# One accumulator instead of two for the sums of the first edge layer

## The reference, cut to what matters

```python
h = (layernorm(x) @ W.T).reshape(N, 8, 32)
alpha = leaky_relu(einsum(h[src], a_src) + einsum(h[dst], a_dst))          # one per edge and head
exp_a = exp(alpha - segment_max(alpha, dst)[dst])
seg_sum = segment_sum(exp_a, dst)
agg = segment_sum(h[src] * (exp_a / max(seg_sum[dst], 1e-10)), dst)
x = x + agg.reshape(N, 256) + bias
x = x + ffn(layernorm(x)); ...
```

## Time and profile before

| what | value |
|---|---|
| median of 3 runs | 1845.91 us (1844.1 to 1847.94) |
| profiled execution, its own time | 1847.34 us |
| its span in the profile | 1845.6 us |
| busy in the span: PE, DVE, ACT, POOL | 1307.0, 1403.1, 935.2, 1085.2 us |
| first edge layer (63 to 640 us): PE, DVE, ACT, POOL busy | 337.0, 477.7, 300.8, 424.1 us |
| Vector's adds in it (L936) | 416 |
| Vector's busy time of 640 to 680 us, the first mixing | 33.5 us |

### The profile page before, as it was taken

The page is one execution under the profiler, slowest core; times in us unless marked ns, Lnnn a source line. Parts: engine busy times, 40 slices in busy tenths (PEclk is TensorE's granted clock), DMA queues, the critical chain, the costliest instruction groups (busy, mean ns, idle before and its releaser), DMA issues. The chain is left out here.

```text
span 1845.6 us, 29221 instructions
## 1 busy us (share of the span) xinstructions
PE 1307.0 (71%) x7043; PEld 921.3 (50%) x7043; DVE 1403.1 (76%) x3587; ACT 935.2 (51%) x3225; POOL 1085.2 (59%) x1146
## 2 busy tenths in 40 slices
PE   6346656665566468999795787877787878867086
PEld 5234434443344366777453455555555555456075
DVE  6558888888889962544867899999999999675444
ACT  3345555545545352332351476777777777346043
POOL 3677777777777200000416777777777777474556
PEclk9668777777777758999997799999999999876588
DMA  5566666667666209200247888888888888436392
GB/s 151 157 186 209 206 215 204 206 208 208 214 205 198 85 1 321 81 1 1 91 171 254 261 262 259 250 267 264 273 263 271 253 270 255 136 114 154 142 333 65
DMA packets 168854, 353.60 MB, mean 192 GB/s; under 512 B 27831, under 2 KB 64776, under 8 KB 168564
## 3 DMA queue, kind: packets, MB, share of 16 engines
q0 software_dynamic: 58192, 175.85, 31.4%
q1 hardware_dynamic: 106501, 172.46, 28.7%
q10 hardware_dynamic: 4000, 3.41, 0.6%
HBM read 268.43 MB, written 87.33 MB: 193 GB/s over the span
## 5 line engine op out<-in xcount | busy, mean ns | idle before, releaser
L827 POOL DMA_INDIRECT e_rows<-h_rows,src_col x416 | 414.8, 997 | 136.8 <-issue 123.4
L1345 POOL DMA_INDIRECT e_rows<-kv_rows,src_col x320 | 307.0, 959 | 101.2 <-issue 67.3
L1104 PE MATMUL e_sum<-e_rows,e_of_dst 128*128 128x264 f32 x832 | 294.5, 497 | 85.6 <-DVE e_rows L926 78.3
L1564 ACT ACTIVATE e_rows<-e_rows 128x64 f32<-128x64 f32 x1152 | 281.4, 336 | 0.3
L1627 PE MATMUL e_query<-q,e_to_dst 128*128 x1248 | 203.6, 295 | 75.1 <-DVE e_rows L1398 56.9
L1104 PEld LDWEIGHTS e_sum<-e_rows,e_of_dst 128*128 128x128 f32 x832 | 177.7, 240 | 126.1 <-DVE e_rows L926 82.2
L1667 PE MATMUL e_sum<-e_rows,e_of_dst 128*128 128x260 f32 x640 | 187.4, 416 | 1.3 <-POOL e_rows L1274 0.7
L1627 PEld LDWEIGHTS e_query<-q,e_to_dst 128*128 128x128 bf16 x1248 | 120.2, 100 | 131.4 <-issue 92.0
L1029 ACT ACTIVATE e_rows<-e_rows 128x32 f32<-128x32 f32 x832 | 181.0, 305 | 0.1
L1486 DVE TENSOR_TENSOR acc<-acc,e_sum 128x260 f32 x346 | 145.5, 420 | 42.1 <-DVE acc L1486 19.4
L1345 POOL DMA_INDIRECT x<-kv_rows,src_col x96 | 91.7, 955 | 73.4 <-POOLq L2149 39.8
(11 more groups left out here) (429 smaller groups left out, 2728.5 us busy)
## 6 DMA issues: line engine op xcount, KB each, us to landing
step_of<-e_of_dst SPq DMA_DIRECT2D x104, 256.0 KB, 2.2
e_of_dst<-step_of SPq DMA_DIRECT2D x104, 256.0 KB
sorted_rows<-zeros SPq DMA_DIRECT2D x1, 14560.0 KB
comb<-sorted_rows SPq DMA_DIRECT2D x56, 260.0 KB
e_rel<-step_rel SPq DMA_DIRECT2D x26, 512.0 KB, 4.3
step_to<-e_to_dst SPq DMA_DIRECT2D x26, 512.0 KB, 5.7
e_to_dst<-step_to SPq DMA_DIRECT2D x52, 256.0 KB
e_rows<-h_rows,src_col POOLq DMA_INDIRECT x416, 3.3
```

Source lines behind the costliest of these rows:

```text
L827: pool.indirect_dma_start(out=g[t // BATCH % R][:, t % BATCH, :], out_offset=None, in_=k.h_rows[:, :], in_offset=bass.IndirectOffsetOnAxis ...
L1104: pe.matmul(psm[t % NB], of_dst[q][:, s % GROUP, :], g[m % R][:, s, :], start=True, stop=True).then_inc(summed, 1)
L1345: pool.indirect_dma_start(out=rows_at(t, 1)[:, 0, :], out_offset=None, in_=k.kv_rows[:, :], in_offset=bass.IndirectOffsetOnAxis(ap=k.src_c ...
L1564: ins = act.activation(x, x, ACT.Copy, scale=row[:, plo + h:plo + h + 1])
```

## The change

`acc0_odd` goes away. `edges_first` gets a list of one accumulator, so it clears and rescales one, all steps are added to it, and `len(accs)` in the wait of `add` is 1: add t waits until add t-1 has ended, where it waited for add t-2. In `mix_first` the two additions per round go away, and the bound reads the sums in the accumulator directly.

```diff
-                c.inc(v.tensor_tensor(inv[b][:, :, :], k.acc0[:, at, D:R0], k.acc0_odd[:, at, D:R0], ALU.add))
-                summed = c.count
-                c.inc(v.tensor_tensor(vals, vals, k.acc0_odd[:, at, 0:D], ALU.add))
-                v.wait_ge(k.dve_steps, summed)
-                c.inc(v.tensor_scalar(inv[b][:, :, :], inv[b][:, :, :], 1e-10, None, ALU.max))
+                c.inc(v.tensor_scalar(inv[b][:, :, :], k.acc0[:, at, D:R0], 1e-10, None, ALU.max))
...
             k.acc0 = sb(stage, "acc0", [P, WIN, R0])
-            k.acc0_odd = sb(stage, "acc0_odd", [P, WIN, R0])
             with ExitStack() as inner:
-                edges_first(nc, k, a, inner, [k.acc0, k.acc0_odd])
+                edges_first(nc, k, a, inner, [k.acc0])
```

## The result

| | before | after |
|---|---|---|
| median, 6 runs each | 1844.7 us | 1854.84 us |
| span of the profiled execution | 1845.6 us | 1854.3 us |
| score row of batch 2 | 128.31 | 129.69 |
| score row of batch 24 | 585.34 | 596.21 |
| first mixing starts | 636.74 | 651.31 |

The kernel is slower: ratio 1.0057, 95% interval 1.0039 to 1.0075, 10.1 us by the medians. It was forecast slower, by 4.5 us to 1850.4. The time lies in the range of 1846 to 1857, in its upper part, and above the 1848.7 to 1853.5 that the prediction called its forecast. In the profiled executions the edge stage ends 14.6 us later and the mixing gives 2.7 back. Of the 11.9 us then open the profiled span keeps 8.7: the stages behind, which the change does not touch, took 3.2 us less in this execution.

The account below looks back on a forecast made before the run. The gathers were taken to set the steady pace, Vector having some air and bounding the end. Edge stage +7.1 us less 2.6 in the mixing gave +4.5 on 1845.9: 1850.4 us, forecast 1848.7 to 1853.5, range 1846 to 1857.

Parts of the forecast that it names:

- steady part: First edge layer, batches 2 to 24: Vector's 456.2 us nearly tie with the gathers' 457.0, so nearly nothing is paid.
- the 2.45 us behind batch 22: After the last full gather wait, two laps without air put batch 24's score row at 587.8 instead of 585.34.
- The new wait: Neighbouring adds into the one accumulator start 0.63 us apart instead of 0.34, costing 0.29 us per direct neighbour.
- rival C: The added waits cost nothing, as the skill says; laps of 18.3 us stay behind the gathers; 1841.5 us; chance 0.08.
- One lap: A Vector lap gains 2.14 us from add waits and loses 0.42 of rescale: 1.72 longer, 20.42 us.
- rival A: Vector becomes the bound outright as idle time before the rescale grows; 1862.6 us, 1854.9 with half; chance 0.15.
- B: Rival: the gathers go on hiding all and only the tail counts; 1847.5 to 1848.7 us; chance 0.20.
- the chance of "slower": Chance 0.53 of measurably slower: two thirds of the forecast's range, lying above the 3.7 us resolution, with rival A.
- The tail: Last laps of the edge stage, where nothing hides Vector: with the 2.45 us before it, the stage ends 7.1 us later.
- the lock (2.8): Tail comparison beside GpSimd's multiplications: an exclusive port lock blocks the loser, so its end moves by 2.8 us.
- the share (3.4): Alternative for the same comparison: Vector and GpSimd share the time, and it ends 0.6 us later, 3.4.
- The mixing: First mixing: five merging additions vanish, two of them on the path, saving 2.6 us (bounds 1.5 to 3.0).

Follow-up runs that it names:

- e1: Kernel before (two accumulators, two rescale pairs, merging additions), but each add waits for the one in front; 1867.55 us, ratio 1.0137.
- e2: Changed kernel with the wait for the add in front put on the add itself, the register operation waiting only for Tensor; 1840.0 us, ratio 0.9981.
- e5: Changed kernel without the five bias additions, so the output lacks the bias; 1847.07 us.
- e7: Changed kernel with the loading of a lap's window registers moved from just before the rescale to the middle of the lap before; 1841.61 us, ratio 0.999.
- e8: Changed kernel with eight small matmuls on Tensor per batch whose results nobody reads; 1853.14 us, ratio 1.0049.
- e4: Kernel before with the strict wait (each add for the one in front) for the adds of batches 24 and 25 only; 1849.65 us, ratio 1.0040.
- e6: Kernel before without the five bias additions, so the output lacks the bias; 1840.37 us, ratio 0.9985.
- e9: Changed kernel with both the wait on the add itself and the window registers loaded in the middle of the lap before; 1842.31 us, ratio 0.9993.
- e10: Kernel before without the first mixing's additions that merge the accumulators, so the odd steps' sums are missing; 1841.89 us, ratio 0.9992.
- e11: Kernel before with each bias addition replaced by a reduction of the same piece, one SBUF input instead of two; 1840.27 us, ratio 0.998.
- e3: Kernel before with the strict wait (each add for the one in front) for the adds of batches 0 to 23 only; 1860.97 us, ratio 1.0100.
- e12: e9 with three of the five bias additions moved into the first mixing, in front of the wait for the square root; 1836.78 us, ratio 0.9957.

## Why the prediction was right, and where its sizes were off

The direction and the range came out, and in part by luck. The step that carries most of the time, a steady part hidden behind the gathers, was wrong: between the rows of batches 2 and 24 nothing was forecast but the 2.45 us behind batch 22, and 9.5 us came. A tail 0.95 us shorter than said and 3.2 us less behind the mixing, for which no term stood in the sum, brought the time back into the range. Of the prediction's signs of being right the spacing and the square root's wait came; batch 24's row near 588 and the mixing 7 us later did not (596.21 and 14.6).

**The new wait: right.** 0.63 a neighbour was taken from the second layer; 0.62 to 0.64 was measured. What "VectorE: DVE Perf Modes" of the Trainium skill, section "The DRAIN you can't avoid", measured on eight copies, that a semaphore costs nothing extra (rival C), does not carry over to these adds: e1, which adds only waits, is 24.0 us slower. e2 shows what the earlier trace rows could not: more than half of it (0.18 of 0.30) is the place of the wait.

**One lap: nearly right as a difference, wrong as a length.** The clean lap, from 171.38 to 191.91, is 20.53 us. By its parts: rescale -0.41 (said -0.42), up to add 9 +1.20 and +0.34 (said +1.47), from there to the end +0.70 (said +0.67). That is 0.11 more than 20.42. But the mean own lap is 20.89. In the kernel before it was 18.98, not the 18.70 that the sum started from: with 18.98 + 1.72 the same sum gives 22 x 20.70 + 7.0 = 462.4 us, 5.4 beyond the gathers and no tie.

**The steady part: this step failed.** "Nearly a tie, and nearly nothing is paid for it": 22 x 20.42 + 7.0 = 456.2 against the gathers' 457.0. Measured were 596.21 - 129.69 = 466.5 us, and batch 24's row moved by 10.9 instead of 2.45; 1.4 of that came in before batch 2, which is within the scatter of that row. The missing 0.47 us a lap are three things:
- 0.11 in the clean lap, above;
- 0.16 of idle time before the rescale. The 18.70 us were read off one lap, that from 295.03, which has nearly the shortest such idle time, 0.49. The mean before was 0.70, and after it is 15.3 / 24 = 0.64, where the clean lap has 0.48. The mean of the earlier trace rows was quoted in rival A and not put into the lap;
- 0.20 that is left: in six of the 22 laps Tensor's last sums come late (the 0.28 and 0.45 above) and cost 0.2 to 0.3 us, in five others one add starts about 0.35 us late, and one lap holds 0.5 us elsewhere.

22 x 0.47 = 10.3 us, less the 0.8 of air that the sum had left: 9.5, the 466.5 - 457.0 that was measured. A term of 0.47 us, multiplied by 22, was more than twice the whole forecast. The absent waits of the score reduction, e5 and e7 show that it is Vector's own time that is paid there, and e8 that a faster Tensor does not give its share back.

Rival A gave 1854.9 us for half of its lengthening, and that is the time measured, by coincidence. Its outcome came, Vector became the bound outright; its mechanism did not: the idle time before the rescale did not grow. It had been there, and stopped being hidden. Two figures of the rivals and chances do not follow from their own terms: B's lower time is 1845.9 + 4.6 - 2.6 = 1847.9, not 1847.5, and some four fifths of 1848.7 to 1853.5, not two thirds, lie above 1845.9 + 3.7, which makes the chance of "slower" 0.61 rather than 0.53.

**The tail: nearly right in sum, its parts off.** From batch 24's score row to the mixing 51.40 us before and 55.10 after: +3.7, said 7.1 - 2.45 = +4.65. The last sixteen adds take 650.55 - 640.94 = 9.61 us against 5.87, +3.7 (said +3.6). The last rescale with what follows takes 640.94 - 638.82 = 2.12 us where it took 630.13 - 626.61 = 3.52: -1.4 (said -1.0, bound -1.3). From batch 25's score row to that rescale it takes 18.22 us where it took 15.84, +2.4 (said +2.1). The lap into batch 25 was to be level and is 1.04 shorter. GpSimd's multiplications begin right behind the probabilities, as said, but Vector meets them later in their run: the comparison took 0.86 us instead of 3.35, and GpSimd went on for 1.9 us beyond it. So neither the lock (2.8) nor the share (3.4) was what happened: it matters where in GpSimd's eight operations the comparison falls. The other kernels agree. In before, e2, e4, e6, e9, e10 and e11 it begins 0.05 to 1.25 us behind GpSimd's first multiplication and ends 4.59 to 4.61 behind it each time, which is the forecast's step; in after, e1, e3 and e8 it begins 2.58 to 2.60 behind and takes 0.85 or 0.86 us. (e7, at 1.75, ends 5.17 behind, and e5, at 2.97, takes 1.06.) The forecast moved GpSimd's work and not Vector's meeting with it.

**The mixing: right.** -2.67 by the trace of after and of e10, said -2.6; the wait in the later rounds 2.31, said 2.3.

**Behind it.** The sum took everything behind the mixing as rigid. In the profiled executions it took 3.2 us less, and no run tells why; the medians' 10.1 lies between 8.7 and 11.9.

## What to carry to other kernels

Where two engines come out within a few per cent of each other, take the mean over all repetitions of the leading lap, idle times included, and not the cleanest lap; 0.5 us times the trip count decides which of them leads. A dependence between neighbours on one engine needs not cost much: look at which instruction carries the wait before you double a buffer to avoid it (e2, 14.8 us below after by one moved wait). And an engine that seems to have air can still slow its neighbour by what it reads; shortening the laps of Vector gave nothing here once the gathers led (e9), moving its two-input operations away did (e12).

## What the runs showed of the hardware

- The same dependence between neighbouring 128x264 adds: 0.34 us from start to start with none, 0.46 with the wait on the add, 0.64 with the wait on the register operation in front of it.
- A gather of GpSimd that starts within a comparison or bias addition of Vector, both with two SBUF inputs, and is lengthened by it, ends 0.80 to 0.84 us behind that operation's end: it takes up to 1.50 us instead of 0.95 in a comparison (e5), up to 2.19 in an addition of 1.48 us (e1). Within a one-input reduction of 1.48 us it is not lengthened (e11).
- A comparison that begins within the first 1.25 us of GpSimd's eight multiplications ends 4.6 us behind their start (seven kernels); one that begins 2.6 us behind their start takes 0.85 or 0.86 us (four kernels).
- The loading of sixteen window registers leaves Vector idle for 0.42 to 1.70 us before the rescale (0.42 in after, 1.70 in e6). Started half a lap earlier it costs nothing that can be seen (e7, e9: no idle time there).
- A shorter wait for Tensor can turn into a longer one for registers (e8): two idle times of one lap are not independent.
